# Quantising the operands of a down product on GpSimd and ScalarE instead of VectorE, in a four-layer transformer kernel

## The reference

```python
def _act_fake_quant(x, clip_factor):
    scale = jax.nn.sigmoid(clip_factor) * jnp.max(jnp.abs(x)) / QMAX
    return jnp.clip(_ste_round(x / scale), -QMAX - 1.0, QMAX) * scale
xq = _act_fake_quant(x, clip_x[0])
gate = jnp.einsum('bsh,ih->bsi', xq, _weight_fake_quant(w_gate))
up = jnp.einsum('bsh,ih->bsi', xq, _weight_fake_quant(w_up))
h = _act_fake_quant(jax.nn.silu(gate) * up, clip_down[0])
return jnp.einsum('bsi,hi->bsh', h, _weight_fake_quant(w_down))
...
# L3: x = x + attention(layernorm(x), ctx) with a causal mask over 16 heads of 8
#     x = x + relu(layernorm(x) @ w1 + b1) @ w2 + b2
```

## Time and profile before

| | |
|---|---|
| median of three runs | 1531.88 us (1530.64 to 1533.39) |
| the profiled execution | 1531.93 us |
| span of its trace | 1530.2 us |
| busy, PE / PEld / DVE / ACT / POOL | 83% / 64% / 70% / 55% / 53% |
| mean granted clock of TensorE | 0.889 |

### The profile page before, as it was taken

The page is one execution under the profiler, slowest core; times in us unless marked ns, Lnnn a source line. Parts: engine busy times, 40 slices in busy tenths (PEclk is TensorE's granted clock), DMA queues, the critical chain, the costliest instruction groups (busy, mean ns, idle before and its releaser), DMA issues. The chain is left out here.

```text
span 1530.2 us, 37250 instructions
## 1 busy us (share of the span) xinstructions
PE 1268.2 (83%) x14512; PEld 979.4 (64%) x14513; DVE 1073.0 (70%) x2505; ACT 849.0 (55%) x2715; POOL 806.9 (53%) x822
## 2 busy tenths in 40 slices
PE   5789879878888888887898888789885588899997
PEld 4677767665767676666666756557463266667776
DVE  4457786886877687877678788987555988655652
ACT  3687666445459458647848546554534334445542
POOL 3038496596476438742864866773223523334332
PEclk7577887998979889998999899999998678999999
DMA  6000000000000000000000000001010000000000
GB/s 160 5 1 1 1 1 1 2 2 1 21 1 1 21 2 1 1 21 2 1 21 2 1 1 10 8 10 45 1 56 19 1 1 2 9 10 9 16 10 15
DMA packets 26695, 19.06 MB, mean 12 GB/s; under 512 B 6520, under 2 KB 24216, under 8 KB 26392
## 3 DMA queue, kind: packets, MB, share of 16 engines
q1 hardware_dynamic: 24936, 15.78, 3.6%
q10 hardware_dynamic: 1584, 0.89, 0.2%
HBM read 12.73 MB, written 3.93 MB: 11 GB/s over the span
## 5 line engine op out<-in xcount | busy, mean ns | idle before, releaser
L1204 ACT ACTIVATE arena<-bank 128x512 f32<-128x512 f32 (+5 forms) x361 | 186.2, 545 | 255.1 <-PE bank L507 70.4
L1605 DVE TENSOR_REDUCE arena<-pair 128x8 f32<-128x1024 f32 (+2 forms) x224 | 241.0, 1096 | 104.9 <-PE pair L557 48.4
L2225 POOL TENSOR_SCALAR_AFFINE_SELECT arena<-arena 128x1024 f32<-128x1024 f32 (+1 forms) x128 | 143.8, 1137 | 290.6 <-ACT arena L1574 153.6
L2280 POOL TENSOR_TENSOR arena<-arena 128x512 f32<-128x512 f32 x160 | 188.5, 1178 | 54.6 <-DVE arena L1722 48.0
L1251 ACT ACTIVATE arena<-pair,arena 77x128 f32<-77x128 f32 x512 | 178.2, 370 | 33.6 <-DVE arena L1605 25.7
L2285 POOL TENSOR_TENSOR arena<-arena 128x512 f32<-128x512 f32 x128 | 178.9, 1397 | 10.0
L502 PE MATMUL bank<-ident 128*128 128x128 f32 x780 | 128.9, 308 | 10.6 <-POOL subscale L2177 4.3
L502 PEld LDWEIGHTS bank<-ident 128*128 128x128 f32 x780 | 112.7, 215 | 28.0 <-issue 11.3
L2301 POOL TENSOR_TENSOR arena<-arena 128x512 f32<-128x512 f32 x64 | 67.7, 1072 | 117.0 <-ACT arena L1204 75.7
L1574 ACT ACTIVATE arena<-pair 77x1024 f32<-77x1024 f32 x64 | 62.3, 1014 | 103.9 <-PE pair L1126 98.8
L1251 ACT ACTIVATION_READ_ACCUMULATOR arena<-pair,arena 77x1 f32 x512 | 108.8, 212 | 0.0
(11 more groups left out here) (294 smaller groups left out, 3064.2 us busy)
## 6 DMA issues: line engine op xcount, KB each, us to landing
arena<-in_ctx_turned SPq DMA_DIRECT2D x16, 154.0 KB, 3.1
arena<-in_x SPq DMA_DIRECT2D x8, 256.0 KB, 4.3
out<-arena SPq DMA_DIRECT2D x8, 256.0 KB, 2.3
spill<-arena SPq DMA_DIRECT2D x7, 256.0 KB, 2.0
arena<-spill SPq DMA_DIRECT2D x7, 256.0 KB, 4.3
arena<-in_ctx SPq DMA_DIRECT2D x8, 154.0 KB
arena<-in_ctx_turned SPq DMA_DIRECT2D x1, 1232.0 KB, 6.0
wexp<-in_L_ffn_expert_w SPq DMA_DIRECT2D x1, 512.0 KB, 4.2
```

The source lines that it names most:

```text
L1204: return act.activation(dst, src, func, bias=bias, scale=scale)
L1605: return dve.tensor_reduce(dst, src, X, op, **kw)
L2225: return pool.affine_select(out=e, in_=e, compare_op=ALU.is_ge, fill=0.0, base=0, pattern=[[0, 8], [1, 128]], channel_multiplier=-1)
L2280: pool.tensor_tensor(into, xvs[:, b, ex * SHD:(ex + 1) * SHD].unsqueeze(1).broadcast_to([128, SH, SHD]), gates[g % 2][:, b, 0:SH, ex].unsq ...
```

## The change

The third to 24th of the 24 tile quantisations leave VectorE. GpSimd does the first two steps of each (`mult`/`add`, then `min`/`max`, both in `hwork`), and ScalarE the last, `copy` with the bias `minusround` = -ROUND, writing bf16. VectorE keeps tiles 0 and 1 of group 0, for which there is a new semaphore `c_first`; `c_clip` goes from GpSimd to ScalarE, and `c_q` is now given by ScalarE. GpSimd starts a group when `c_q` says that ScalarE has read the one before out of `hwork`; ScalarE waits for the down product two groups back before it writes `hqs`. The four strings of stage C in `ORDER` are written anew. `FILL` stays as it is. One small `memset` is added among the constants of stage A, and `vector` signals `ainv_ready` a second time.

```diff
-NCONST, NLATER = 11, 19
+NCONST, NLATER = 11, 20
...
     ("C", "vector"):
-        "aaaabaaababbaccaacdcaadaaccbaaeacdceaccaaadcacaadeaacceaefccdbeaadbccafedcfcadefcceebfbdccefcdcefdcc"
...
+        "aaabbabccccdaccdedccababccedccedacceefccdabbdeccfefdccfecdceaefcdcdcfceebfdccbecdcefefcdcbbedccffecc"
...
     ("C", "gpsimd"):
-        "bbddbddddddddfddfddbddddfbddddfddddfddddfdbdddfddbddfddddfddddfbddddfdddddfdddfddfddddff",
+        "aaabaaaabaaaddaaadaaddadbaddaaddfaafdadddbdddfdddfddddbddfdddbdfddddfddddfddbddfddfddbddddfddddfdddd"
+        "fdddddfdff",
...
-        silu_table = gmax[:, 1:2]
+        silu_table, minusround = gmax[:, 1:2], gmax[:, 3:4]
...
# TensorE
                 keep(o, "down0")
+                if g == 0:
+                    pe.wait_ge(c_first, 1)
                 pe.wait_ge(c_q, C.next(c_q))
...
# ScalarE
+            def down(g):
+                for t, (r0, m) in enumerate(ITILES):
+                    if g == 0 and t < 2:
+                        continue
+                    yield
+                    if t == 0 and g >= 2:
+                        o = E["down", g - 2]
+                        act.wait_ge(o.full, o.n)
+                    act.wait_ge(c_clip, C.next(c_clip))
+                    ins = copy(hqs[g % 2][0:m, t, :], hwork[0:m, t, :], bias=minusround[0:m])
+                ins.then_inc(C.give(c_q), 1)
...
# VectorE
             act_scale(1)
+            dve.drain().then_inc(ainv_ready, 1)
 
             def down(g):
                 x = x3[g]
-                for t, (r0, m) in enumerate(ITILES):
-                    yield
-                    if t == 0 and g >= 2:
-                        o = E["down", g - 2]
-                        dve.wait_ge(o.full, o.n)
-                    if t == 0 and g:
-                        dve.wait_ge(c_q, g)
-                    ins = quantise(hqs[g % 2][0:m, t, :], h_all[0:m, t, g * W:(g + 1) * W], ainv[0:m, 1:2], hwork[0:m, t, :])
-                ins.then_inc(C.give(c_q), 1)
                 if g == 0:
+                    for t in range(2):
+                        yield
+                        ins = quantise(hqs[0][:, t, :], h_all[:, t, 0:W], ainv[:, 1:2], hwork[:, t, :])
+                    ins.then_inc(c_first, 1)
...
                 o = E["down", g]
                 dve.wait_ge(o.full, o.n)
+                if g:
+                    dve.wait_ge(c_added, g)
...
# GpSimd
+            def down(g):
+                for t, (r0, m) in enumerate(ITILES):
+                    if g == 0 and t < 2:
+                        continue
+                    yield
+                    if g == 0:
+                        pool.wait_ge(ainv_ready, 2)
+                    if g and t == 0:
+                        pool.wait_ge(c_q, g)
+                    if g == 1 and t == 0:
+                        pool.wait_ge(c_first, 1)
+                    w = hwork[0:m, t, :]
+                    pool.tensor_scalar(w, h_all[0:m, t, g * W:(g + 1) * W], ainv[0:m, 1:2], ROUND, ALU.mult, ALU.add)\
+                        .then_inc(C.give(pool_step), 1)
+                    pool.wait_ge(pool_step, C.last(pool_step))
+                    pool.tensor_scalar(w, w, ROUND + QMAX, ROUND - QMAX - 1.0, ALU.min, ALU.max).then_inc(C.give(c_clip), 1)
```

More of the change, by code:

```diff
@@ L51 @@
     ("C", "tensor"):
-        "ababcbdcabddceaddcecaddceaddcebbadedceddfcefffdfdcaeddfcedebdcbedfdffcedffdcfdedcedbedcbedfdcfefdfdf"
-        "ceddfcebddebceddfceffdfdfceddfcedebdcbedfdcffeddffcfdedcebdedbceddfcedffdfcefddfcededcedfdfffdedfdef"
+        "ababcacdbddbceddacadedcecddacedebdcbadedfcffdefdfcedfdceadedcbbddfefcfedfdfcedfcdededbcbedfdcfffdefc"
+        "dfdecdeddebcefdbdffcedffdceddfcedbedbddefcffcffdedfdedcecbddecedfbffcdeddffceddfcededcedfdfdeffdfdef"
         "eeffffff",
@@ L65 @@
     ("C", "scalar"):
-        "bbbbbbbddbddddddbbbbddfddfffddddbbddbbfdfdfddfddbbddbbfddffddfddbbbddbddfffddfddbbddbbfddffddfddbbbd"
-        "dbfddfdfdfddddffddffddddffff",
+        "baaababbaaabbaaabddaaddabddaaaaddbbaddbabdfdffdaadfaddbbddbfbdfdfddfddbbddbbfddffdfdddbbddbffddbfddf"
+        "ddbbddbdfdfbfdfdddbbbddfdfbdfddfddddfdfdfdddfdffff",
     ("A", "vector"):
@@ L79 @@
     ("C", "vector"):
-        "aaaabaaababbaccaacdcaadaaccbaaeacdceaccaaadcacaadeaacceaefccdbeaadbccafedcfcadefcceebfbdccefcdcefdcc"
-        "feccdeebfcdceccdeffcdcbefcdceebdccfbdeccefdfccdfecceefcdcdeccfedbfcbcdfeccebedfcceccdedfccefdfcceefd"
-        "ccedfdfeeefeffff",
+        "aaabbabccccdaccdedccababccedccedacceefccdabbdeccfefdccfecdceaefcdcdcfceebfdccbecdcefefcdcbbedccffecc"
+        "defcdcebefdccefccdebcdcfedfcceefdbedbccccffedfdccecceefdccefcdcdefccdbeccefefcdcedefdfefeeffff",
     ("A", "gpsimd"):
@@ L421, in four_layers @@
         ainv_ready = sem("ainv_ready")
-        c_q, c_xb, c_added = sem("c_q"), sem("c_xb"), sem("c_added")
+        c_q, c_first, c_clip, c_xb, c_added = sem("c_q"), sem("c_first"), sem("c_clip"), sem("c_xb"), sem("c_added")
         y_stored = [sem(f"y_stored{i}") for i in range(2)]
@@ L1588, in f3 @@
                     act.activation(hid[:, t, :], o.bank[:, 0:W], ACT.Relu, bias=b31[:, t:t + 1]).then_inc(o.drained, 1)
-            merge(ORDER["C", "scalar"], {"b": x3p, "d": x3t, "f": f3})
+            merge(ORDER["C", "scalar"], {"a": down, "b": x3p, "d": x3t, "f": f3})
         @block.vector
@@ L2213, in constants @@
                 then(pool.memset(vpad, 0.0))
+                then(pool.memset(minusround, -ROUND))
                 then(pool.memset(nmG, 0.0))
@@ L2404, in f3 @@
                 pool.tensor_tensor(x, x, b32.unsqueeze(1).broadcast_to([128, SEQS, CH]), ALU.add).then_inc(C.give(c_xb), 1)
-            merge(ORDER["C", "gpsimd"], {"b": x3p, "f": f3} | ({"d": x3t} if "x3" in POOL_MASK else {}))
+            merge(ORDER["C", "gpsimd"], {"a": down, "b": x3p, "f": f3} | ({"d": x3t} if "x3" in POOL_MASK else {}))
         @block.sync
```

## The result

The changed kernel took 1512.54 us in the median of four runs (1499.72 to 1514.99), against 1532.64 us; the ratio is 0.985, 95% interval 0.981 to 0.990. Measured again beside other runs of the kernel before it was 0.986 (0.981 to 0.991). The profiled execution took 1514.99 us, its span 1513.3 us. The forecast was 11 us less. The medians differ by 20.1 us, the ratio stands for 23 (16 to 29), and the part of the program that was changed gained 17.7, as follows: the direction was right, and the size was about half to two thirds of what came. (The ratios in this document leave out executions more than 1.5% above the fastest of their kernel.)

What follows compares the result with a forecast made beforehand. It took VectorE's full queue, with TensorE's waits paid again at half clock, to bound early stage C. Group 1's output product 11 us earlier and 0 afterwards gave 1531.93 - 11 = 1520.9, said as 1521 us, range 1512 to 1529.

Steps and rivals of the forecast that it cites:

- The ceiling: Rival: TensorE's work alone bounds stage C's start, all 22 us lost there go, 1510 us; chance 0.14.
- early stretch: Stage C from 1240 to 1322 us: VectorE 79% busy, TensorE's mean clock 0.81, about 22 us lost against later.
- The mark: Group 1's output product on TensorE, at 1321.3 us before, forecast at 1310, 11 us less.
- the walk: Following stage C's queues engine by engine in the new order, through group 0's value products to group 1's output product: 1310 us.
- the middle: The forecast itself: 11 us less for the whole kernel; its band of 7 to 15 us less had chance 0.55.
- The mechanism: Stage C, 1240 to 1322 us: VectorE's queue, 79% busy, holds up the maxima; without the tiles it has 40 us of work.
- were never work: Of some 36 us of tiles leaving VectorE, some 10 us were instructions stretched beside GpSimd's.
- The start: Ahead of stage C's first down product: two tiles on VectorE beside one on GpSimd and ScalarE, saving 1 us.
- The rest of the order: From group 1's output product on: same TensorE work at full clock, 0 us gained, with 3 us either way.
- The tiles in the masks' way: GpSimd's in-order queue: a mask waits for up to three tiles, 4.4 us, ahead of it.
- The rule against the change: VectorE and GpSimd share an SBUF port, so moving work between them might not help; one instruction stretched from 0.43 to 1.20 us.
- The slower rival: Rival: stage C's tiles stand in series with the masks at half clock, 6 us more, 1538 us; chance 0.07.

Runs made afterwards that it cites:

- the one without the clip: Changed kernel without GpSimd's `min`/`max` instruction on its 22 tiles: 301.3 us from the reciprocal to the end (changed kernel 300.5), ratio 0.987 to before.
- move alone: Kernel before with GpSimd and ScalarE quantising 22 tiles, but stage C's old order kept: 324.6 us from reciprocal to end (before 318.2), ratio 1.005.
- order alone: Kernel before, VectorE quantising all 24 tiles, with the changed kernel's stage C order: 322.4 us from reciprocal to end (before 318.2), ratio 1.003; tiles re-placed, 321.1 us.
- the doubled clip: Changed kernel with GpSimd's `min`/`max` made twice on each of its 22 tiles: 313.3 us from reciprocal to end (changed kernel 300.5), ratio 1.003 to before.

## Why the prediction was wrong

**The ceiling: right.** The early stretch was found to lose 22 us against the later one. The mark came 19.6 us earlier, counted from the reciprocal (18.8 from the span's start). That the median, 1512.54 us, still lies at the edge of the stated range of 1512 to 1529 is no merit of the walk: the gain to the mark was put at 11 us.

**The step that failed: the walk from the second value product on.** It put TensorE at half clock there ("3.65 us for both halves at half clock", and score product and transposes likewise), since the kernel before ran so in the earlier trace rows. The changed kernel never fell to the lower level between 1240.8 and 1302.5 us. Measured value products against the walk: 1242.6 (1242), 1252.7 (1252 to 1254), 1257.7 (1260), 1267.7 (1269); output products 1271.1 (1274) and 1302.5 (1310). Up to the second product the walk holds within 1 us. From there to the mark it has 57 us, and 49.8 were measured. The parts: 7 us forecast and 5.0 measured, 9 and 9.9, 5 and 3.4, 36 and 31.4. In the second of them two waits of TensorE, 1.64 us for the maxima and 1.05 us for the exponential, took the place of the slow matmuls. The largest miss is the last one: "TensorE may fall to half clock once more; at 35 to 36 us". It was 31.4 us. The prediction had itself written that a wait of TensorE is paid twice, and then took away the waits and kept the slow matmuls. Had the walk been made at the full clock, the ceiling of 22 us would have been nearer than the middle; it had been given 0.14. That the clock held was not certain beforehand: it did in both traces of the changed kernel, and fell for 7 us in the one without the clip, behind the same wait.

**The mechanism: half right.** The reason given was that VectorE is full and its queue holds up the maxima. By itself that is not enough: with the move alone VectorE was emptied and the kernel slower. The old order makes the scores behind the previous value product, TensorE waits for the exponential again and again and falls to half clock (before: 0.81; move alone: 71.54 us busy at 0.78); holding the clock by fills gave 4.0 us. The new order only works if the operands are there in time (order alone: up to 12.2 us of waits for VectorE's tiles), and that is what the move gives. So both halves are needed: 4 us lost with the order alone, 6 lost with the move alone, 17.7 gained with both. Open is how much of the 6 is the old order and how much the place of ScalarE's copies, and whether VectorE's load would bind the old order at the full clock. VectorE's own numbers: its 40 us of work came as forecast (40.95), but in a shorter stretch, 66% of it and not below 60%. And of the tiles' time on VectorE 7 us, not 10, "were never work": 16 full tiles at 1.79 us against 1.35 (0.49 + 0.43 + 0.43). Neither number stood in the sum.

**Prices.** GpSimd 0.697 and 0.615 us forecast; 0.70 to 0.82 and 0.62 to 0.67 measured, about 1.5 with the gaps. ScalarE's copy 0.75 forecast, 0.72 measured. The start 1 us forecast; first down product 3.67 us behind the reciprocal against 4.30, so 0.6. The rest of the order 0, within 3: it gave 1.9 back.

**The tiles in the masks' way: right as a place, wrong as a price.** Around the second and third products masks do stand behind tiles. Taking a third of the tiles away changed nothing, taking the clip off all of them next to nothing, and a second clip on each cost 12.8 us. The longest single wait with the doubled clip was not for a mask but for ScalarE (3.69 us, ahead of the query product), whose copies the prediction took as hidden except ahead of an exponential.

**The rule against the change.** It names a real effect: VectorE's adding of the down product went from 0.692 to 0.924 us in the mean (8 times 0.23, 1.9 us), and tiles on VectorE beside masks from 1.3 to 2.4 us. The Trainium skill (Perfetto Trace Analysis, Optimizing Scalar/DVE Operations) says that offloading between these two "might not help". The measurement decides: with the old order it did not help, for reasons that are in part open, and with the new one it did. That what still collides stands off the path is argued, not shown.

**The slower rival** did not come. With 15 us more on GpSimd stage C was 12.8 us longer than in the changed kernel, still 4.9 us shorter than before, and the ratio was 1.003.

## What to carry to other kernels

Where TensorE waits a little in every round, work out its time at the clock that the new pattern of waits would give, not at the clock that the old trace shows: here some two thirds of the gain was the same matmuls at the other level. Allow for both levels where waits of about 2 us remain, since the same wait kept the clock in one trace and lost it in another. A reordering and an offload can each be worth nothing or less and be worth 17.7 us together; before giving up one, make the other's condition true. When an offload is tried in an old order, look where the receiving engines' new steps stand: here two copies stood ahead of an exponential. And look at an engine's price on both sides: GpSimd's instruction was worth next to nothing to remove and cost most of its length to add.

## What was not expected of the hardware

- The part ahead of stage C, which is the same in all 14 traces but for one small `memset`, varied between 1198.6 and 1218.5 us, while the 300.5 us of the changed kernel behind it repeated within 0.1 us.
- Five small matmuls in each of eight waits held TensorE's clock at 1.00 (2.4 GHz) over 75 us in which it had been at 0.81 in the mean; with the move in place, where waits of up to 5.80 us were left, the same fills held it at 0.88 only.
- The changed kernel's TensorE was granted 1.00 from 1240.8 to 1302.5 us although its waits there still come to 6.9 us; in the kernel before, with 12.4 us of waits in 82, it was at 0.81 in the mean, so it fell to the lower level (1.2 GHz) again and again, though none of its waits was over 2.0 us.
- Behind the same steps and the same wait of 2.15 us TensorE stayed at 1.00 in the changed kernel and fell to 0.50 for some 7 us in the kernel without the clip.
